# Block scores from 64-row products in pairs, in a layer-norm, Taylor, SwiGLU and block-winner kernel

## The reference, cut to what matters

```python
x = _layernorm(x + taylor(x) + (silu(x @ gate.T) * (x @ up.T)) @ down.T)
inter = xf @ c1_w.T @ c2_w.T                  # 512 -> 16 -> 1792 scores
blk = inter.reshape(B * T, 56, 32)
idx = jnp.argmax(blk, axis=-1) + jnp.arange(0, 1792, 32)
h = relu(einsum('bkm,bm->bk', w1[idx], xf))   # one of 32 rows in each block
out = einsum('bk,bkm->bm', h, w2t[idx])
x = _layernorm(x + out)
```

## Time and profile before

| | |
|---|---|
| median of 3 runs | 745.96 us (745.2 to 746.12) |
| the profiled execution | 745.69 us, its span 743.5 us |
| TensorE busy in the span | 724.3 us, 97% |
| VectorE busy | 477.9 us, 64% |
| ScalarE busy | 212.8 us, 29% |
| GpSimd busy | 155.8 us, 21% |
| granted TensorE clock, mean | 0.996 of full |

### The profile page before, as it was taken

The page is one execution under the profiler, slowest core; times in us unless marked ns, Lnnn a source line. Parts: engine busy times, 40 slices in busy tenths (PEclk is TensorE's granted clock), DMA queues, the critical chain, the costliest instruction groups (busy, mean ns, idle before and its releaser), DMA issues.

```text
span 743.5 us, 10579 instructions
## 1 busy us (share of the span) xinstructions
PE 724.3 (97%) x3431; PEld 331.1 (45%) x3431; DVE 477.9 (64%) x916; ACT 212.8 (29%) x340; POOL 155.8 (21%) x132
## 2 busy tenths in 40 slices
PE   6999999999999999999999999999999999999994
PEld 2444444444444444444444444444444444444442
DVE  4887687697877789688868879653665361125115
ACT  1645367444721211112122111222212222122210
POOL 0433452211111111111111111222212222122210
PEclk9999999999999999999999999999999999999998
DMA  9438309410000000100004350105110005001001
GB/s 328 180 115 267 56 1 340 113 38 20 1 14 16 17 15 3 28 16 16 1 16 88 51 106 6 25 2 100 56 30 2 1 20 137 1 1 57 1 1 56
DMA packets 35374, 43.53 MB, mean 59 GB/s; under 512 B 19974, under 2 KB 27782, under 8 KB 34438
## 3 DMA queue, kind: packets, MB, share of 16 engines
q1 hardware_dynamic: 33222, 38.78, 17.6%
q0 software_dynamic: 2112, 4.19, 3.4%
HBM read 34.33 MB, written 4.44 MB: 52 GB/s over the span
## 4 chain that ended last, share of the span: by engine, by line
PE 84%; DVE 8%; issue 3%; DMA 2%; ACT 1%; SPq 1%; ACTq 0%; DVEq 0%; POOL 0%
PE acc L454 28%; PE pb L440 20%; PE pa L440 20%; PE acc L519 10%; DVE sc L1365 2%; DVE big L1033 1%; PE acc L737 1%; DMA big<-in_x_t 1%; DVE big L1357 1%; DVE work L1229 1%; PE pick_a L502 1%; ACT big L881 1%; PE pick_a L573 1%; PE pick_b L573 1%; DVE small L1246 1%
## 5 line engine op out<-in xcount | busy, mean ns | idle before, releaser
L454 PE MATMUL acc<-big,work 128*128 128x512 f16 x1104 | 248.4, 379 | 0.0
L942 POOL TENSOR_TENSOR work<-work 128x512 f32 (+1 forms) x96 | 112.3, 1172 | 503.4 <-ACT work L861 275.4
L440 PE MATMUL pa<-xs,big 128*128 128x512 f16 x816 | 188.9, 379 | 0.7 <-DVE work L1229 0.7
L440 PE MATMUL pb<-xs,big 128*128 128x512 f16 x816 | 187.2, 379 | 0.0
L454 PEld LDWEIGHTS acc<-big,work 128*128 128x128 f16 x1104 | 107.7, 98 | 128.3
L440 PEld LDWEIGHTS pb<-xs,big 128*128 128x128 f16 x816 | 78.6, 98 | 91.6
L440 PEld LDWEIGHTS pa<-xs,big 128*128 128x128 f16 x816 | 78.0, 98 | 90.7 <-issue 1.2
L919 ACT ACTIVATE work<-work 128x512 f32 x56 | 35.1, 628 | 219.6 <-DVE work L1470 216.6
L1470 DVE SCALAR_TENSOR_TENSOR work<-big,const_sb,pa 128x512 f32<-128x512 f16 (+1 forms) x28 | 20.9, 745 | 83.2 <-PE pa L440 83.0
L519 PE MATMUL acc<-big 128*128 128x512 f16 x336 | 73.7, 379 | 0.6 <-POOL big L949 0.6
L861 ACT ACTIVATE work<-work 128x512 f32 (+1 forms) x40 | 25.2, 630 | 157.7 <-DVE work L1229 157.7
(11 more groups left out here) (140 smaller groups left out, 512.8 us busy)
## 6 DMA issues: line engine op xcount, KB each, us to landing
big<-in_w_all SPq DMA_DIRECT2D x2, 3840.0 KB, 16.8
big<-spread_rows SPq DMA_DIRECT2D x16, 448.0 KB, 7.6
big<-in_x_t SPq DMA_DIRECT2D x16, 256.0 KB, 4.1
rows<-in_x POOLq DMA_DIRECT2D x4, 1024.0 KB, 10.9
big<-in_w_all SPq DMA_DIRECT2D x2, 1536.0 KB, 10.3
out<-rows SPq DMA_DIRECT2D x3, 1024.0 KB, 5.0
big<-in_w_all SPq DMA_DIRECT2D x1, 2048.0 KB, 16.1
big<-in_w_all SPq DMA_DIRECT2D x2, 1024.0 KB, 5.2
```

The source lines that it names most:

```text
L440: mm = nc.tensor.matmul(dst[:, :], weights(wp)(kc * P, P), x_part16(g, xp, kc), start=(kc == 0 and wp == xp), stop=(kc == KC - 1 and wp == 1))
L454: mm = nc.tensor.matmul(acc[t][:, :], act_part(pair, j, ap, t * P, P), weights(wp)(0, H), start=(first and ap == wp), stop=(last and ap == 1))
L942: nc.gpsimd.tensor_tensor(act_part(pair, j, 1), act32[j], act_part(pair, j, 0), ALU.subtract).then_inc(act_lo, 1)
```

## The change

The scores get along with half the rows. z is cut in two float16 pieces and c2 in two, so their four cross products with 16 ranks each are 64 rows. `z_stack` holds this set twice, on rows 0 to 63 and 64 to 127. `c2_stack` is half as wide (896 columns): its lower 64 rows hold the columns of k = 0 and 2, its upper 64 those of k = 1 and 3. A score product then uses only one half of the rows, lower for even k and upper for odd, and the program built from it gives it as such to TensorE (a tile of 64 rows by 128 columns, at row 0 or at row 64).

```diff
-                nc.tensor.matmul(dst[:, 0:PICK_COLS], z_stack, c2_stack[:, k * PICK_COLS:(k + 1) * PICK_COLS],
+                half = slice(k % 2 * (P // 2), (k % 2 + 1) * (P // 2))
+                at = k // 2 * PICK_COLS
+                nc.tensor.matmul(dst[:, 0:PICK_COLS], z_stack[half, :], c2_stack[half, at:at + PICK_COLS],
                                  start=True, stop=True).then_inc(score_ready, 1)
```

k = 2 moves to stand directly ahead of k = 3, so that a tile has two pairs, and in phase 2 k = 3 follows k = 2 in the same place:

```diff
-                    if tile is not None:
-                        if j == 0:
-                            turn_z(tile, pick_a)
-                        else:
-                            scores(tile, 2, pick_a)
+                    if tile is not None and j == 0:
+                        turn_z(tile, pick_a)
...
                     if j == 0 and scored is not None:
+                        scores(scored, 2, pick_a)
                         scores(scored, 3, pick_b)
...
                     if i == 0:
-                        unit2(g, 1, s(tile - 1, 3), none, none, "first")
-                    unit2(g, 2 * i + 2, s(tile - 1, 3) if i else none, none, none, "middle")
+                        unit2(g, 1, none if g else s(tile - 1, 3), none, none, "first")
+                    unit2(g, 2 * i + 2, s(tile - 1, 2, 3) if i else none, none, none, "middle")
                     unit2(g, 2 * i + 3, none, zt(tile), s(tile, 0, 1), "middle", between=z2(tile, GROUPS - 1, g * 2 + i))
-                    s(tile, 2)()
-                unit2(g, 6, none, none, none, "middle")
+                unit2(g, 6, s(tile, 2, 3), none, none, "middle")
```

VectorE's order follows, and z is cut in two instead of three:

```diff
                 pick(tile, 1, pick_b)
+                swiglu(g, u, 1)
                 pick(tile, 2, pick_a)
-                swiglu(g, u, 1)
...
-                step(v.tensor_copy(pieces(0, 3), wide(z_sum, 3)))
-                settle()
-                step(v.tensor_tensor(z_rest, z_sum, z_split[:, 0:RANK], ALU.subtract))
-                settle()
-                step(v.tensor_copy(pieces(3, 3), wide(z_rest, 3)))
+                step(v.tensor_scalar(pieces[:, :, 0], wide, Z_SCALE, None, ALU.mult))
                 settle()
-                v.tensor_tensor(pieces(6, 2), wide(z_rest, 2), pieces(3, 2), ALU.subtract).then_inc(z_cut, 1)
+                v.scalar_tensor_tensor(out=pieces[:, :, 1], in0=wide, scalar=Z_SCALE, in1=pieces[:, :, 0],
+                                       op0=ALU.mult, op1=ALU.subtract).then_inc(z_cut, 1)
```

```diff
-                        peaks(g + 2, [x_part[:, g + 1:g + 2], t_part[:, g + 1:g + 2]], delta_bank(g))
+                        peaks(g + 2, [x_part[:, g + 1:g + 2], t_part[:, g + 1:g + 2]] + ([c2_part] if g == 2 else []), delta_bank(g))
...
+                if g == 3:
+                    power_scales(peak[:, 2:3], c2_exp, c2_scale, c2_inv, c2_scaled)
...
-                    rest_c2()
+                    max_c2()
...
-                elif g == 3 and m == 2:
+                elif g == 3 and m in (2, 3, 5):
+                    w1_max({2: 3, 3: 4, 5: 5}[m])
+                elif g == 3 and m == 4:
                     stack_c2()
-                elif g == 3 and m in (3, 4, 5):
-                    w1_max(m)
```

More of the change, by code:

```diff
@@ L25 @@
 F16 = mybir.dt.float16
-BF16 = mybir.dt.bfloat16
 I32 = mybir.dt.int32
@@ L71 @@
 X1_SCALE = 2.0 ** 9
+Z_SCALE = 2.0 ** -17
+HALF_COLS = F2 // 2
 HID_SCALE = 2.0 ** -17
 CONST_COLS = 5 + SPARSITY + P
-PEAK_PARTS = (2, 3, 5, 7, 9, 10, 11)
+PEAK_PARTS = (2, 3, 5, 7, 10, 11, 12)
 PEAK_X1, PEAK_W1, PEAK_W2 = 2, GROUPS + 1, GROUPS + 2
@@ L121, in program @@
         work32 = work[:, :].bitcast(F32)
-        c2_stack = sb("c2_stack", [P, F2], BF16)
+        c2_stack = sb("c2_stack", [P, HALF_COLS], F16)
         c1_parts = sb("c1_parts", [P, KC * 2 * RANK], F16)
@@ L125, in program @@
         ident16 = sb("ident16", [P, P], F16)
-        ident_bf = sb("ident_bf", [P, P], BF16)
         rev_wide = sb("rev_wide", [P, PICK_COLS], F16)
@@ L129, in program @@
         disc_sb = sb("disc_sb", [P, G], F32)
-        sc = sb("sc", [P, 64], F32)
+        sc = sb("sc", [P, 68], F32)
         small = sb("small", [P, 44], F32)
-        c2_later, c2_last = [const_sb[:, i:i + 1] for i in (2, 3)]
+        c2_later = const_sb[:, 2:3]
+        c2_part, c2_exp, c2_scale, c2_inv = [sc[:, i:i + 1] for i in range(64, 68)]
         c1_hi_part, c1_lo_part = [c1_parts[:, :].rearrange("p (k a r) -> p k a r", k=KC, a=2)[:, :, a, :] for a in range(2)]
@@ L204, in spare_x @@
             return xs[:, g * 2 * KC * GT + a:g * 2 * KC * GT + a + n]
-        c2_raw = spare_x(GROUPS - 2, 0, 2 * F2).bitcast(F32)
+        c2_raw = spare_x(GROUPS - 2, 0, 2 * HALF_COLS).bitcast(F32)
         c1_raw = spare_x(GROUPS - 1, 0, 2 * KC * RANK).bitcast(F32).rearrange("p (k r) -> p k r", k=KC)
-        c2_round = spare_x(GROUPS - 1, 2 * KC * P, F2).bitcast(BF16)
+        c2_high = spare_x(GROUPS - 1, 2 * KC * P, HALF_COLS)
         a32 = AUX_AT
@@ L214, in program @@
         z_sum, z_rest = words(a32 + H, RANK), words(a32 + H + RANK, RANK)
-        z_split = big16[:, a16 + 256:a16 + 384].bitcast(BF16)
-        z_stack = big16[:, a16 + 512:a16 + 640].bitcast(BF16)
+        z_split = big16[:, a16 + 256:a16 + 384]
+        z_stack = big16[:, a16 + 512:a16 + 640]
         hit = [big16[:, a16 + 640 + i * PICK_COLS:a16 + 640 + (i + 1) * PICK_COLS] for i in range(2)]
@@ L272, in program @@
         delta_ready, terms_ready, banks_added = sem("delta_ready"), sem("terms_ready"), sem("banks_added")
-        term_scaled, fuse_scaled, c2_rest = sem("term_scaled"), sem("fuse_scaled"), sem("c2_rest")
+        term_scaled, fuse_scaled, c2_scaled = sem("term_scaled"), sem("fuse_scaled"), sem("c2_scaled")
         max_part, x_scaled, w_scaled, xlo_ready = sem("max_part"), sem("x_scaled"), sem("w_scaled"), sem("xlo_ready")
@@ L560, in turn_z @@
                 pe.wait_ge(z_cut, tile + 1)
-                nc.tensor.transpose(dst[:, :].bitcast(BF16)[:, 0:P], z_split, ident_bf[:, :])
+                nc.tensor.transpose(dst[:, :].bitcast(F16)[:, 0:P], z_split, ident16[:, :])
                 turn_winner(tile, dst)
@@ L714, in _ @@
                     if i == 0:
-                        unit2(g, 1, s(tile - 1, 3), none, none, "first")
-                    unit2(g, 2 * i + 2, s(tile - 1, 3) if i else none, none, none, "middle")
+                        unit2(g, 1, none if g else s(tile - 1, 3), none, none, "first")
+                    unit2(g, 2 * i + 2, s(tile - 1, 2, 3) if i else none, none, none, "middle")
                     unit2(g, 2 * i + 3, none, zt(tile), s(tile, 0, 1), "middle", between=z2(tile, GROUPS - 1, g * 2 + i))
-                    s(tile, 2)()
-                unit2(g, 6, none, none, none, "middle")
+                unit2(g, 6, s(tile, 2, 3), none, none, "middle")
                 unit2(g + 1, 0, none, none, none, "last")
             for g in (2, 3):
-                unit2(g, 1, s(GROUPS * TPG - 1, 3) if g == 2 else none, none, none, "first")
+                unit2(g, 1, none, none, none, "first")
                 if g == 2:
@@ L804, in terms_high @@
                         x_hi(1, 1)
-                    if g == 2 and m == 5:
-                        act.wait_ge(c2_rest, 1)
-                        act.activation(c2_round, c2_raw, ACT.Copy).then_inc(c2_cast, 1)
+                    if g == 3 and m == 3:
+                        act.wait_ge(c2_scaled, 1)
+                        act.activation(c2_high, c2_raw, ACT.Copy, scale=c2_scale).then_inc(c2_cast, 1)
+                        act.wait_ge(c2_cast, 1)
+                        act.activation(c2_high, c2_high, ACT.Copy, scale=c2_later).then_inc(c2_cast, 1)
                     if g == 3 and m == 2:
@@ L1004, in small_constants, with max_c2 @@
                 step(v.tensor_copy(ident16[:, :], ident32))
-                step(v.tensor_copy(ident_bf[:, :], ident32))
                 step(v.tensor_copy(rev_wide[:, :].rearrange("p (b j) -> p b j", j=SPARSITY), rev32.unsqueeze(1).broadcast_to([P, PB, SPARSITY])))
[L1008 to L1012, removed]
+            def max_c2():
+                dve.wait_ge(c2_in, 16)
+                v.tensor_reduce(c2_part, c2_raw, axis=AX.X, op=ALU.max, apply_absolute_value=True).then_inc(max_part, 1)
             def stack_c2():
                 dve.wait_ge(c2_cast, 2)
-                v.scalar_tensor_tensor(out=c2_stack[:, :], in0=c2_round, scalar=c2_last, in1=c2_raw,
+                v.scalar_tensor_tensor(out=c2_stack[:, :], in0=c2_raw, scalar=c2_scale, in1=c2_high,
                                        op0=ALU.mult, op1=ALU.add).then_inc(c2_stacked, 1)
@@ L1119, in scale_terms @@
                 else:
-                    peaks(g + 1 if g else 0, 2, delta_bank(g - 1) if g else acc[TPG - 1])
+                    peaks(g + 1 if g else 0, 3 if g == 3 else 2, delta_bank(g - 1) if g else acc[TPG - 1])
                 power_scales(peak[:, 0:1] if g == 1 else peak[:, 1:2], t_exp[:, g:g + 1], t_scale[:, g:g + 1], t_inv[:, g:g + 1], t_scaled)
@@ L1326, in stack_z @@
                 dve.wait_ge(winner_turned, tile + 1)
```

(18 more changed lines are left out.)

8 lines of the change are left out of this document (2 added, 6 removed).

## The result

| | before | changed |
|---|---|---|
| median of 13 runs each | 745.94 us | 748.26 us |
| lowest and highest | 744.71, 747.76 | 746.19, 750.02 |
| span of the profiled execution | 743.5 us | 746.4 us |

The ratio is 1.0029, with an interval of 1.0021 to 1.0037: the changed kernel is slower by 2.2 us (1.6 to 2.8). I had forecast 741.5 and faster. In a second series of 12 runs the ratio was 1.0026 (1.0014 to 1.0038). Two executions of the kernel before in a later series, 772.11 and 1296.39 us at a granted clock of 0.947 and 0.558, are left out of all ratios and counts here.

What follows compares the result with a forecast made beforehand. TensorE, busy 724.3 of 743.5 us, was taken to bound the kernel through distances between matmul starts. Terms -5.3 + 1.3 + 0.2 - 0.7 = -4.5 us gave 741.5 us, 0.6% faster; range 739.5 to 754.

Steps and rivals of the forecast that it cites:

- I take 0.02 us a change, 1.3 us in all: TensorE's 66 switches between 128-row and 64-row products: 0.02 us each, 1.3 us in all, with 0 and 0.26 as bounds.
- My break-even: Cost of one switch between 128-row and 64-row products above which the prediction fails: about 0.09 us.
- rival 1: Every change of form empties TensorE's array, at 0.16 or 0.26 us each: 750.8 or 757.4 us; chance 0.37.
- rival 2: Pairs run one after the other, changes free, 745.5 us; or a drain eats the gain, 743.5 to 746.5; together 0.13.
- The pairs: Two scores on different row halves of TensorE run side by side, 0.02 us stagger: 31 x 0.17 = 5.3 us won.
- The swap: SwiGLU product moved ahead of pick 2 on VectorE: TensorE's wait at phase 2's start goes, -0.7 us.
- The third peak product: Group 3's peaks get a third product on TensorE with nothing else running there meanwhile: +0.2 us.
- Term 4's low part: In group 3, c2's preparation makes this term 1.5 us later; room shrinks from 3.2 to 1.7 us, so hidden.
- `cut_z`: VectorE step in a scoring unit: 3 steps in about 0.65 us instead of 5 in 1.1, keeping a 0.4 to 0.5 margin.
- the thin margin: Score 3 needs bank `pick_b` back: 0.06 to 0.11 us left; if missed, under 1 us lost in all.
- the mask behind both picks: In phase 2 pick 3 stands ahead of the masks; mask ends near 581.3, bank wanted by 583.33: hidden, 1.8 us to spare.

Runs made afterwards that it cites:

- experiment 1: Changed kernel with each score product over all 128 rows, so no 64-row products: 745.24 us, ratio 0.9993 to the kernel before.
- experiments 3: Changed kernel with phase 1's third score back ahead of the down products, giving one pair and two lone scores in 11 tiles: 751.38 us, ratio 1.0077.
- 10: Changed kernel with tile 11's third and fourth scores made a pair too: one run, 746.93 us; phase 2's stretch 288.60 instead of 288.99 us.
- Experiments 7: Kernel before with three tiny unused copies more in VectorE's program, in group 3 of the Taylor stage: 745.99 us, ratio 1.0011.
- 9: Changed kernel with 19 tiny copies more in VectorE's program in the last group: one run, 748.32 us; tail 20.11 instead of 20.47 us.
- experiment 8: Changed kernel as it is, for a second profile and more times: 747.23 us, ratio 1.0026 to the kernel before.
- experiment 6: Changed kernel with c2's half stack loaded twice, the second copy unused: 746.92 us, ratio 1.0020; the changed kernel beside it 747.23.
- experiment 5: Changed kernel with each of phase 1's 22 pairs multiplied twice in a row, four 64-row products a visit: one run, 752.97 us.

## Why the prediction was wrong

**The step that failed** is "I take 0.02 us a change, 1.3 us in all". Three ways of measuring give the same other number. The gaps of 0.10 on each side of a pair are in the timeline; experiment 1 against the changed kernel gives 0.50 us for 22 pairs, 0.02 more than two 128-row scores, and 0.63 - 9 x 0.02 = 0.45, about 0.2 for each of the two lone ones; experiments 3 and 10 give 0.40 for a visit that holds one score. So a visit costs 0.21 us and 33 visits 6.9 us. I had reasoned from changes of type and of kind, which are free and came out free again (the float16 transposes and scores of experiment 1). They say nothing on a change of rows. My break-even was 0.09 us a change, and it came to 0.10: the mechanism is that of rival 1, at the size of the second half of rival 2 ("about 0.07 to 0.11 us and eats the gain"), to which I gave, with its other half, 0.13. Rival 1 with its own prices, 0.16 or 0.26 a change, did not happen. What fills the 0.10 us stays open: it is less than the full way through the array (0.16 us), and it is also about as long as one weight load (0.09), which is no longer done ahead; no run separates the two.

The Trainium skill, "TensorEngine Tiling (Array Packing)", Key Properties, says that changing the tiling mode drains TensorE. The trace agrees in that a change costs 0.10 us; that it is a drain, no row shows by itself. The Trainium skill, "TensorE: Matmul & The Clock Gate", Part 3, has products on different row groups run at once, about 4 ns apart; here they start 0 to 0.01 us apart. The two rules hold together, and I gave the first too little weight against the second.

**The pairs**: side by side, as forecast, with no stagger. 31 x 0.19 = 5.9 us won where I had 5.3. The changes lost more, 6.9: the two stretches against experiment 1 give +1.1 us (0.50 + 0.63) instead of my -4.0.

**The swap** of the SwiGLU product and pick 2: the pause is gone, -0.9 us where I had -0.7. The idle time of 0.75 in the profile understates the stall by the 0.16 us by which the last product's time outlasts its distance to a follower.

**The third peak product**: +0.19, forecast 0.2.

**What had to stay hidden did.** Term 4's low part ends at 105.40 and is read at 107.35, 1.9 us of room (forecast 1.7). `cut_z` takes 0.67 to 0.69 us (0.65). Bank `pick_b` was free in time: at all 33 visits the first score starts 0.10 us late behind the product in front, pair or lone, and nowhere more. The pairs did not make the unit shorter, so the thin margin was not put to the test. In phase 2 the mask behind both picks ends at 583.62 and its bank is wanted at 586.01, 2.4 us of room (1.8).

**What I left out** are two pauses of VectorE, 0.47 us in the conversions and 0.36 us in the tail, on the path both times. I had priced what the new instructions do, and put at nothing where the later ones stand. Experiments 7 and 9 show that the pauses come and go with instructions added ahead, one of them in the old kernel. That the engine waits for its own instructions there is my reading; no row names it.

**The sum**: +1.13 - 0.91 + 0.19 + 0.47 + 0.36 = +1.24 us, the 1.25 of the table. The times say 2.2 (1.6 to 2.8) and 1.9. What is left, under 1 us, goes with the late start: 14 of 25 executions of the changed kernel have it and 8 of 49 of the kernel before, which at 1.4 to 1.6 us each is about 0.5 us (an estimate from the table of experiment 8). It also accounts for most of what experiment 1, with 0 of 11, gained in the times (2 to 3 us) beyond the 1.1 of the stretches. Whether the change makes the late start more frequent stays open: side by side on one chip it was 5 of 12 for the changed kernel and 4 of 27 for the one before, with the full load of c2 (experiment 6) 1 of 12, and experiment 1, which has the halved load, had none. The groups are far apart when pooled, but these counts don't tell which part of the change would do it, if any does.

The better version is the old kernel with the swap alone, 744.31 us: it has the one part of the change that paid, without 64-row products.

## What to carry to other kernels

Products on half the rows do run side by side, but a visit from full-row work costs 0.2 us, as much as the 448-column product that a pair saves. So one pair a visit wins nothing. Two pairs took 0.59 us (experiment 5), where four full-row products of this size take 4 x 0.19 = 0.76; a gain from that, or from longer products, is an estimate that no kernel here puts to use. A lone half-row product cost 0.40 us where a full-row one costs 0.19. Before giving a type or kind of change the price nought, ask whether the rows of the trace changed the same thing; a bound of 0 to 0.26 with the break-even at 0.09 deserved its middle, not its lower end. When a wait is the only thing that a rewrite cures, try the one line that cures it by itself.

## What the hardware showed that I had not expected

- A change between 128-row and 64-row products costs 0.10 us each way, and no weights are loaded ahead over it (the load starts within 0.01 us of its product, and 0.21 us ahead without a change); inside the 64-row form products follow at 0.19 us and on both halves at once.
- Three tiny copies added to VectorE's program broke a run of eight later instructions and cost 0.44 us; nineteen others removed a pause of 0.36 us. Both were on the path.
- Between 16 and 26 us the same program had TensorE at 2.4 GHz throughout in one execution and in part at 1.2 GHz in another, which cost 1.2 us, after idle times of 1.25 and 3.37 us. The idle time doesn't decide it alone: experiment 10 had 3.02 us and kept its clock, experiment 9 had 1.91 and lost it.
